# A graph and attention network on one core: the normalised features stay in SBUF, and the first loop turns them from there, one step ahead

## The reference

```python
xn = _layernorm(x, axis=-1)
x = x + _L0_gnn_ref(xn, src, dst, edge_weight, ...) + _L0_mix_ref(xn[None], ...)[0]

# _L0_gnn_ref: xn @ W_self + segment_sum((xn @ W_neighbor)[src] * weight, dst) + bias
# _L0_mix_ref:
qkv = x @ W_qkv + b_qkv
q, k, v = jnp.split(qkv, 3, axis=2)      # q and k less their means
k2 = _l2_normalize(k * k / (k2s + EPS_DIV), axis=-2)   # over the nodes
q2 = _l2_normalize(q * q / (q2s + EPS_DIV), axis=-1)
kv = jnp.einsum('bnc,bnd->bcd', k2, v)
attn = v + jnp.einsum('bnc,bcd->bnd', q2, kv) / math.sqrt(N)
return attn @ W_out + b_out
```

## Time and profile before

| what | before |
|---|---|
| median of 3 runs | 3417.4 us (3412.79 to 3418.47) |
| the profiled execution | 3412.11 us, of this a span of 3410.5 us |
| busy: PE / DVE / ACT / POOL | 2484.1 / 1166.1 / 1083.1 / 587.4 us |
| PE busy from 0 to 50, 50 to 100, 100 to 150, 150 to 200 us | 0.00, 3.04, 26.12, 14.71 us |
| PE busy from 500 to 550 us | 47.62 us |
| first instruction of the graph sums' stage on DVE | 454.33 us |
| mean granted TensorE clock | 0.838 of full speed (2.4 GHz; the lower level of 1.2 GHz stands as 0.50) |

### The profile page before, as it was taken

One profiled execution on the slowest core, in us unless ns is written; L12 is line 12 of the kernel. 1 busy time (PEld: TensorE's weight loads), 2 busy tenths in 40 slices (PEclk: granted clock), 3 DMA queues, 4 the chain that ended last, 5 costly groups with the idle time before them and its releaser, 6 DMA issues.

```text
span 3410.5 us, 39172 instructions
## 1 busy us (share of the span) xinstructions
PE 2484.1 (73%) x11905; PEld 1986.4 (58%) x11906; DVE 1166.1 (34%) x2489; ACT 1083.1 (32%) x1985; POOL 587.4 (17%) x482
## 2 busy tenths in 40 slices
PE   0455579987967869787489926588787877853887
PEld 0223368876756757666378814366565655642776
DVE  3233357765253544532100043202333233221111
ACT  2312157775544445542133321001111111111222
POOL 1222001010010010102112100131212121212544
PEclk9777669999879789897689968798788878776999
DMA  3222011111011010112322132321212112023443
GB/s 109 72 91 80 34 41 41 40 47 39 27 43 37 24 56 28 42 37 82 94 77 74 53 116 100 88 65 33 70 42 73 51 52 62 25 73 87 82 93 63
DMA packets 168994, 208.46 MB, mean 61 GB/s; under 512 B 59830, under 2 KB 137399, under 8 KB 168860
## 3 DMA queue, kind: packets, MB, share of 16 engines
q0 software_dynamic: 75168, 89.11, 11.3%
q1 hardware_dynamic: 80342, 88.80, 8.1%
q10 hardware_dynamic: 13350, 28.87, 2.4%
HBM read 114.91 MB, written 93.74 MB: 61 GB/s over the span
## 4 chain that ended last, share of the span: by engine, by line
PE 57%; DMA 15%; another core or an unknown queue 14%; DVE 4%; SPq 3%; ACT 3%; issue 3%; ACTq 0%; DVEq 0%; POOL 0%; POOLq 0%
PE bank L708 53%; DMA agg_rows<-agg_t 8%; PE bank L714 4%; DMA arena<-agg_rows 3%; DMA counts<-count_a 1%; SPq L478 1%; ACT t L1099 1%; SPq L395 1%; SPq L471 1%; DMA rows_b<-arena 0%; SPq L476 0%; DMA out_rows<-arena,ids_cur 0%; DVE arena L1824 0%; DMA w_qc<-counts 0%
## 5 line engine op out<-in xcount | busy, mean ns | idle before, releaser
L708 PE MATMUL bank<-xg,w_adj 125*125 125x256 f32 (+1 forms) x2500 | 664.6, 405 | 10.7 <-POOLq L71 10.7
L708 PE MATMUL bank<-arena,row_hot 128*125 128x100 f32 x3200 | 448.8, 289 | 115.3 <-remote 70.9
L708 PEld LDWEIGHTS bank<-arena,row_hot 128*125 128x125 f32 x3200 | 443.5, 206 | 152.0 <-issue 130.5
L708 PEld LDWEIGHTS bank<-xg,w_adj 125*125 125x125 f32 x2500 | 463.8, 198 | 77.0 <-issue 11.9
L714 PE MATMUL bank<-ident,arena 125*128 125x125 f32 x700 | 158.4, 351 | 409.2 <-remote 307.0
L714 PEld LDWEIGHTS bank<-ident,arena 125*128 125x128 f32 x700 | 95.8, 174 | 469.3 <-issue 464.6
L708 PE MATMUL bank<-t,w_h 128*128 128x250 f32 (+1 forms) x1184 | 329.6, 432 | 16.2 <-remote 10.6
L1137 ACT ACTIVATE w_adj<-bank 125x200 f32<-125x200 f32 x400 | 213.3, 533 | 334.7 <-PE bank L708 324.8
L1505 DVE TENSOR_TENSOR row_hot<-iota_all,arena 128x2000 f32<-128x2000 f32 x100 | 223.9, 2239 | 270.2 <-PE bank L708 263.9
L708 PEld LDWEIGHTS bank<-t,w_h 128*128 128x128 f32 x1184 | 232.4, 202 | 110.4 <-issue 58.7
L708 PE MATMUL bank<-w_adj,arena 128*125 128x256 f32 x1024 | 241.8, 394 | 0.0
(11 more groups left out here) (312 smaller groups left out, 2989.7 us busy)
## 6 DMA issues: line engine op xcount, KB each, us to landing
sorted_in<-pad_rows POOLq DMA_DIRECT2D x16, 878.4 KB, 16.8
arena<-sorted_in SPq DMA_DIRECT2D x49, 251.0 KB
counts<-count_a ACTq DMA_DIRECT2D x13, 781.2 KB
count_a<-counts POOLq DMA_DIRECT2D x13, 781.2 KB, 7.7
counts<-w_qc ACTq DMA_DIRECT2D x12, 781.2 KB
w_qc<-counts POOLq DMA_DIRECT2D x12, 781.2 KB, 6.1
arena<-rows_b SPq DMA_DIRECT2D x5, 1875.0 KB
w_adj<-in_L_ffn_Wd POOLq DMA_DIRECT2D x8, 1024.0 KB
```

The lines of the kernel that those rows point to most:

```text
L708: return pe.matmul(o, w, r, start=first, stop=last, skip_group_check=not check)
```

## The change

The normalisation writes into `xg` instead of in place; the scratch of the tables moves from `xg` to `w_adj`, and the ones in `xg`'s last column are written at POOL's start. `feat0` is still stored, from `xg`, but neither the steps' rows nor `xg` are loaded from it. `l_x` becomes five semaphores, one a slice. SP issues the tables' stores ahead of the weights. PE turns a step's rows out of `xg` during the step before it (`t4` has four planes, two for each of two steps) and works on the next step's first two blocks ahead of this step's sums. DVE takes the first guesses before the loop, finds the first edges in step 0, and makes one group of slots after each of steps 1 to 4 and one at the end. The copy of `tail_n` moves from the preparation to `dense_or_tails`. The loop of the normalisation is written out.

```diff
-CSR = {3: (0,), 4: (1, 2), 5: (3, 4)}
+CSR = {1: (0,), 2: (1,), 3: (2,), 4: (3,), 5: (4,)}
...
         def scratch(rows, at, n):
-            return xg[0:rows, at:at + n, :].rearrange("p a b -> p (a b)")
+            return w_adj[0:rows, 257 * at:257 * (at + n)]
...
+            take(sp, tables_made)
+            sp.dma_start(tile_min, st_min[:, :]).then_inc(tables_stored, 16)
+            sp.dma_start(tile_max, st_max[:, :]).then_inc(tables_stored, 16)
             sp.dma_start(wqkvs[:, :, 0:3 * D], wview(a["L0_mix_W_qkv"])).then_inc(l_w0, 16)
...
-            take(sp, tables_made)
-            sp.dma_start(tile_min, st_min[:, :]).then_inc(tables_stored, 16)
-            sp.dma_start(tile_max, st_max[:, :]).then_inc(tables_stored, 16)
             sp.wait_ge(tables_stored, 32)
...
-                sp.dma_start(fv[:, G * i:G * i + G, :], x_big[:, G * i:G * i + G, :]).then_inc(feat0_stored, 16)
+                sp.dma_start(fv[:, G * i:G * i + G, :], xg[:, G * i:G * i + G, 0:D]).then_inc(feat0_stored, 16)
...
-            sp.wait_ge(feat0_stored, 80)
 
             def x_rows(s):
                 take(sp, xa_used)
-                sp.dma_start(y, rows(feat0, s)).then_inc(xa_in, 16)
                 sp.dma_start(x1, rows(a["x"], s)).then_inc(xa_in, 16)
...
-            take(sp, xf_full)
-            sp.dma_start(xg[:, 0:NB, 0:D], by_part(feat0)).then_inc(xf_full, 16)
...
+            def heads(s, i):
+
+                if i < 2 or s == 0:
+                    pe.wait_ge(t_full, i + 1)
+                if i == (G - 1 if s == 0 else 2):
+                    pe.wait_ge(t_full, G)
+                    pe.sem_clear(t_full)
+                at = lambda c: t4[:, 2 * (s % 2) + c, B * i:B * i + B]
+                take(pe, h_free[i % 2])
+                for c in range(KC):
+                    last = mm(ps_h[i % 2][0:B, :], at(c), wqkvs[:, c, 0:512], c == 0, c == 1)
+                last.then_inc(h_dve[i % 2], 1)
+                take(pe, y_free[i % 2])
+                for c in range(KC):
+                    last = mm(ps_y[i % 2][0:B, :], at(c), wqkvs[:, c, 512:1024], c == 0, c == 1)
+                last.then_inc(y_dve[i % 2], 1)
+
+            turn_rows(xg[0:B, 0:G, :])
+            heads(0, 0)
+            heads(0, 1)
             for s in range(NS):
-                take(pe, v_full)
-                turn_rows(y)
-                for i in range(G):
-                    turned(i)
...
+                for i in range(2, G):
+                    heads(s, i)
+                    if s < NS - 1 and i == (G - 1 if s == 0 else 2):
+                        turn_rows(xg[0:B, G * s + G:G * s + 2 * G, :])
+                if s < NS - 1:
+                    heads(s + 1, 0)
+                    heads(s + 1, 1)
 
                 take(pe, k4_full)
...
+            copy_turned(2)
             for s in range(NS):
-                copy_turned(2)
+                if s < NS - 1:
+                    copy_turned(2, 2 * ((s + 1) % 2))
...
-            with dve.Fori(0, NS) as s:
-                for i in range(G):
-                    last = dve.bn_stats(bn6[:, i, :], flat(x_big[:, ds(s * G + i, 1), :]))
+            for s in range(NS):
+                dve.wait_ge(l_x[s], 16)
+                for i in range(G):
+                    last = dve.bn_stats(bn6[:, i, :], x_big[:, s * G + i, :])
...
-                    last = ts(rows_i, rows_i, mv[:, i, 0:1], rs[:, i:i + 1], ALU.subtract, ALU.mult)
+                    last = ts(xg[:, s * G + i, 0:D], x_big[:, s * G + i, :], mv[:, i, 0:1], rs[:, i:i + 1],
+                              ALU.subtract, ALU.mult)
...
-            dve.wait_ge(tables_loaded, 64)
-            chain(dve.tensor_copy(n_f[:, :], tail_n[:, :]))
...
-                take(dve, xa_in, 32)
-                dve.sem_inc(v_full, 1)
...
                 dve.sem_inc(act_in, 1)
+                take(dve, xa_in, 16)
                 chain(tt(row_a[:, :, 0:D], row_a[:, :, 0:D], x1, ALU.add))
...
-                if s == 0:
-                    first_tiles_of()
...
-                if s == 1:
+                if s == 0:
                     first_edges_of()
...
+            first_tiles_of()
             for s in range(NS):
                 attend0(s, s < NS - 1)
```

More of the change, by code:

```diff
@@ L268, in program @@
         t_min, t_max, t_msk, t_val, t_iot = (range_t[:, NT * i:NT * i + NT] for i in range(5))
-        l_x, l_edge, l_w0, l_wh, l_l1, l_c, l_bc, l_b1 = (
-            sem(n) for n in ("x_loaded", "edges_loaded", "w_mix0_loaded", "w_hid0_loaded", "w_layer1_loaded",
+        l_edge, l_w0, l_wh, l_l1, l_c, l_bc, l_b1 = (
+            sem(n) for n in ("edges_loaded", "w_mix0_loaded", "w_hid0_loaded", "w_layer1_loaded",
                              "w_c_loaded", "biases_c_loaded", "b1_loaded"))
+        l_x = [sem(f"x_loaded{s}") for s in range(NS)]
         const_full = sem("consts_made")
@@ L291, in program @@
         adj_in, adj_used = pair("adjacency_in"), pair("adjacency_used")
-        xf_full, graph_done, tables_free = sem("features0_loaded"), sem("graph_summed"), sem("projections_done")
+        graph_done, tables_free = sem("graph_summed"), sem("projections_done")
         l_w1 = sem("w_qkv1_loaded")
@@ L394, in _ @@
             for i in range(5):
-                sp.dma_start(x_big[:, 5 * i:5 * i + 5, :], xv[:, 5 * i:5 * i + 5, :]).then_inc(l_x, 16)
+                sp.dma_start(x_big[:, 5 * i:5 * i + 5, :], xv[:, 5 * i:5 * i + 5, :]).then_inc(l_x[i], 16)
+            take(sp, tables_made)
+            sp.dma_start(tile_min, st_min[:, :]).then_inc(tables_stored, 16)
+            sp.dma_start(tile_max, st_max[:, :]).then_inc(tables_stored, 16)
             sp.dma_start(wqkvs[:, :, 0:3 * D], wview(a["L0_mix_W_qkv"])).then_inc(l_w0, 16)
@@ L538, in _ @@
             chain(pool.tensor_copy(ident_b[:, :], ident[:, :]))
+            chain(pool.memset(xg[:, :, D:D + 1], 1.0))
             chain.restart()
@@ L552, in _ @@
             take(pool, first_tiles)
-            chain(pool.memset(xg[:, :, D:D + 1], 1.0))
-            chain.restart()
-            pool.sem_inc(xf_full, 1)
             tiles = a["dst"].rearrange("(t e) -> t e", e=B)
@@ L895, in _ @@
             zero(ps_kv, 512, True, False)
-            for s in range(NS):
-                take(pe, v_full)
-                turn_rows(y)
-                for i in range(G):
-                    turned(i)
-                    take(pe, h_free[i % 2])
-                    for c in range(KC):
-                        last = mm(ps_h[i % 2][0:B, :], at(c, i), wqkvs[:, c, 0:512], c == 0, c == 1)
-                    last.then_inc(h_dve[i % 2], 1)
-                    take(pe, y_free[i % 2])
-                    for c in range(KC):
-                        last = mm(ps_y[i % 2][0:B, :], at(c, i), wqkvs[:, c, 512:1024], c == 0, c == 1)
-                    last.then_inc(y_dve[i % 2], 1)
+            def heads(s, i):
[16 more added lines that the diff above has]
+            heads(0, 1)
+            for s in range(NS):
+                for i in range(2, G):
[5 more added lines that the diff above has]
+                    heads(s + 1, 1)
                 take(pe, k4_full)
@@ L945, in _ @@
             pe.wait_ge(tabs_ready, 2)
-            pe.wait_ge(xf_full, 16)
             first_adjacency()
@@ L1093, in _, with copy_turned @@
             chain = Chain(act, act_s)
-            def copy_turned(n):
+            def copy_turned(n, k=0):
                 for i in range(G):
                     take(act, t_act[i % 2])
-                    chain(act.activation(t4[:, 0:n, B * i:B * i + B],
+                    chain(act.activation(t4[:, k:k + n, B * i:B * i + B],
                                          ps_t[i % 2][:, 0:n * B].rearrange("p (k n) -> p k n", k=n), ACT.Copy))
@@ L1605, in dense_or_tails @@
             def dense_or_tails():
+                dve.wait_ge(tables_loaded, 64)
+                chain(dve.tensor_copy(n_f[:, :], tail_n[:, :]))
                 chain(dve.tensor_reduce(covered[:, NB:NB + 1], covered[:, 0:NB], AX.X, ALU.add))
```

2 lines of the change are left out of this document (removed).

## The result

The changed kernel takes 3335.2 us (median of 4 runs, 3330.04 to 3344.69) against 3415.1 us (4 runs, 3408.39 to 3418.47): a ratio of 0.977, 95% interval 0.974 to 0.980. The forecast was 3340 (3318 to 3366). The profiled execution took 3344.69 us, 3343.1 of it span. The graph sums' stage, which began at 454.33 us, now begins at 377.11, **77.2 us sooner**; the forecast's sum was 77.0, at 377.3.

A forecast was written before the change was run, and what follows sets the result against it. Up to 454 us a chain through all engines binds, TensorE mostly waiting. Start -29.5, copies +2.4, step 1 -30.7, steps 2 and 3 +8.0 each, step 4 -10.7, tail -24.5: 77.0 us saved, 3340 us forecast (3318 to 3366).

The forecast's parts named there:

- T(1): End of step 1's heads, forecast at 160.5 us; T(s) is the same for step s.
- Start: Up to the first heads: earlier tables' stores and no DRAM wait begin them at 93.3 us, 29.5 us earlier.
- The rival of stores that land no earlier: Tables' stores: loads ahead are as slow on all paths, the start loses 11.0 us, total 3351; chance 0.08.
- Copies ahead of the squares: Step 0: ScalarE copies step 1's turned rows before its squares, a loss of 2.4 us.
- Step 1's wait: Between step 0's sums and step 1's third block: TensorE waits for first edges until 145.0; by places -30.7 us.
- the rival of slower fetches: Edge lists: POOL's fetches take twice 37.5 us, first edges late by that, total 3377; chance 0.04.
- A step: Loop step with one slot group: 52.3 us, of which 15.5 is three blocks' heads, transposes and 2.4 slow start.
- The rival of 28 us: Heads ahead not hidden: banks freed late, sums pushed up to 7.0 us in four steps, total 3368; chance 0.07.
- The rival of a clock that holds: Sums: shorter pause keeps TensorE's clock high, up to -21 us over four steps, total 3319; chance 0.11.
- The transposes: Rival: transposes between heads lower the clock, slow start twice in four steps, +9.6 us, total 3350; chance 0.07.
- Tail: From T(4) to the graph sums' stage: fourth group at 345.5, a further group 12.1 us, stage at 377.3; -24.5 us.
- The stage behind: Everything after the graph sums' stage begins: unchanged at 2956 us.

The follow-up runs named there:

- e10: Changed kernel with the copy of the tail table back in the preparation, ahead of the weights' folding: stage start 381.2 us, median 3347.7 us, ratio 0.9809 to before.
- e1: Changed kernel with the stores of the two small tables back behind the seven weight loads: stage start 386.4 us, median 3346.8 us, ratio 0.9820 to before.
- e5: Kernel before with one edit, the two small tables' stores issued ahead of the seven weight loads: stage start 441.9 us, median 3405.1 us, ratio 0.9978.
- e3: Changed kernel with first edges found in step 1, slot groups behind steps 2, 3, 4 and two at the end: stage 367.0 us, median 3326.0 us.
- e8: Changed kernel with step 0's rows turned first, first guesses in step 0, first edges in step 1, all slots last: stage 357.6, median 3324.3 us.
- e2: Changed kernel with the next step's first two blocks issued behind this step's sums and slots: stage start 395.4 us, median 3359.6 us, ratio 0.9852 to before.
- e9: Changed kernel with 11 unread TensorE products filling each pause ahead of the sums, 27 in the last step: stage 384.0 us, median 3351.2 us.
- e12: e8 with 6 unread filling products in each pause ahead of the sums, 14 in the last: stage start 360.6 us, median 3321.3 us, ratio 0.9734 to before.
- e4: Changed kernel with one group of slots behind step 3, two behind step 4, two at the end: stage start 375.4 us, median 3329.5 us.
- e6: Changed kernel with the order of before, keeping only rows turned from SBUF, the late tail copy and the written-out loop: stage 398.8 us, median 3353.4 us.
- e11: e8 with the filling products of e9 (11 in each pause, 27 in the last): stage start 365.5 us, median 3322.5 us, ratio 0.9735 to before.

## Why the prediction was right

The mechanism was right, and the sum was right to 0.2 us at the stage's start, by steps that were right to some 2 us each. The 0.2 is luck, and so is a median within 5 us when executions scatter by 15: the steps' errors, up to 2.2 us late at T(1), cancelled. By its own steps:

- **Start: 93.3 forecast, 93.98 measured.** Two errors cancel. The stores landed 1.6 us later than I took (34.34 for 32.7): the last slice was issued by 21.2, but the first small store was then held at the queue for 5.24 us, and its landing came 7.7 us after the second's issue. Against it, the written-out loop of the normalisation takes 6.38 us a step (40.72 - 34.34), the loop before 6.8 (50.51 - 43.70); I had priced that part of the change at nothing, and by it ScalarE's count began 29.5 us behind the first normalisation instead of 31.1. The count ended at 90.98 (forecast 90.9), and the first copy began 0.6 us behind it, where I had taken nothing. ScalarE bound: VectorE waited 4.29 us for its count, and by e10 it had 3 us to spare (3.3 forecast). The rival of stores that land no earlier is out by e1 and e5.
- **The Trainium skill, "DMA: Bandwidth & Descriptors" (Why a DMA increments its semaphore by 16 and not by 1).** I had taken its rule on the engines, 5 of 16 for 125 rows, as speaking against a start before 32 us. The start at 34.3 agrees with that, and so does the mean busy share of the 16 transfer engines while only the slices moved, 0.34 from 6 to 26 us, which is 5.4 engines. No row shows whether it was the engines or the queue that held the stores.
- **Copies ahead of the squares, +2.4.** T(0) to the sums was 15.1 us (128.13 - 113.0), forecast 14.7.
- **Step 1's wait.** POOL's fetches ran from 92.89 to 130.70 (forecast 93.1 to 130.6), so the rival of slower fetches is out. The landing took 5.3 us after that, not 3.7, and the first heads behind it came at 147.25 instead of 145.0. The mis-sized term is the landing. e3 shows what this part of the change costs: 10 us.
- **A step: 52.3 forecast.** T(s) is here the start of the 32 rows and half of their 13.90 us, in step 4 the end of its 24 rows. T(1) to T(2) was 52.2, T(2) to T(3) 51.4. T(4) was 314.9, forecast 314.7: what step 1 came late was recovered by 0.9 us in step 3 and in step 4. The mis-sized term is the slow start: 2.4 us in step 1 as forecast, but 1.4, 1.2 and 1.2 in steps 2 to 4 (5.07, 4.91 and 11.73 us for rows that take 3.69 and 10.56 at full clock in e3 and e8).
- **Heads ahead are hidden.** The sums began 12.4 to 12.9 us after T in steps 1 to 4. e2 gives 6.7 us a step for the cover, forecast 7.0. The rival of 28 us is out.
- **The clock.** It had fallen to 0.50 at the sums in all five steps. The rival of a clock that holds was right in what it would do to the rows, and e9 makes it happen, but behind the pause of 5.4 us the clock was as low as behind the longer one. Its 21 us were too many: of its four steps, step 0 could give nothing, because TensorE stood behind its sums for the first edges anyway, and e9 gives some 15 us for the other sums, the last step's among them. No run shows how much would be left in this kernel with the filling at its right size; in e12, which has no slots in its loop, `row_a`'s store took the gain.
- **The transposes.** They ran at full clock (0.43 us a pair) and the 16 or 32 rows behind them at 1.00, in steps 0 to 3; step 4 turns nothing. So the rule of the Trainium skill, "TensorE: Matmul & The Clock Gate" (Part 4: PE-mode transpose), that transposes do not count for the clock as matmuls do, did nothing here in 2.6 us of transposes between heads; the slow start that I counted came once a step, ahead of the transposes: behind the wait for the first edges in step 1 (6.04 us for 8 rows that take 3.69), behind the slots' pauses from step 2 on (5.07 and 4.91).
- **Tail.** T(4) to the fourth group was 30.6 us (30.8), the next group 11.2 (12.1), from there to the stage 20.5 (19.7).
- **The stage behind.** I had said that I am wrong if it takes another time than 2956. It took 2966.0 in the profiled execution, and the other three executions had spans of 3328.5 to 3333.9, which with the same stage start leaves 2951 to 2957. Lined up instruction by instruction, TensorE is 77 to 78 us ahead of before up to 1095 us, 70 to 74 from 1300 to 2860 and 67 at the end. One of these steps can be read. From 1347.3 us TensorE runs 80 products with 8 columns (`wg`); they took 12.3 us before and 15.2 in the changed kernel, at a lower granted clock. They took 12.2 to 12.6 in e1, e4 and e10 too and 15.0 to 15.4 in the other nine, and the four executions with 12.2 to 12.6 are those with the shortest part behind (2955.8 to 2957.4; e3, with 15.4, follows at 2957.6). What decides which clock these rows get wasn't settled. The other steps go both ways from kernel to kernel, and I count them as scatter. Windows over the `wg` rows, before and in the changed kernel (the granted clock is the last number but two):

```profile
1347.30:1359.60 12.30, 12.30 (x82) 12.24 (x81) 5.01 (x4) 0.47 (x2) 1.82 (x2) 0.71 0.26 87
1273.00:1288.20 15.20, 15.20 (x82) 15.13 (x81) 4.94 (x4) 0.47 (x2) 1.82 (x2) 0.57 0.21 71
```

- **Sums and bounds.** The range of the forecast alone should read 3327 to 3359 by its own bounds, not 3325 to 3358, and a clock of 0.805 gives 3434, not 3430. Neither touches the forecast.

The parts nearly add up. From the kernel before it is 55.6 us to the resident rows (e6, with the moved tail copy and the written-out loop), from there 9.3 for the stores (e1) and 18.3 for the heads ahead (e2); the first edges in step 0 take 10.1 back (e3) and the groups of slots spread over the steps 2.7 (e4). That makes 70.4 of the 77.2. What is left lies in the first guesses and the turning done earlier, which no run separates, and in the place where the clock falls, by which e5 alone gained 3 us.

Of the versions tried, e8, e11 and e12 have the lowest ratios: the stage begins 11.6 to 19.5 us before the changed kernel's, and the medians are 11 to 14 us lower, but the intervals of the ratios overlap with the changed kernel's. That they are faster than it is shown for the stage's start and only likely for the total.

## What to carry to other kernels

Price a change along the one chain that ends last, and then look at what is next on it: filling the pause made the sums of e12 2 to 5 us shorter a step, and the store of a single-buffered tile took it back. A piece of work that is moved earlier must be checked against the transfer it waits for: the first edges, moved one step ahead, stood in front of their own data. And where executions scatter by more than the effect, compare the time of one marked instruction in the traces before comparing medians.

## What the runs showed of the hardware

- In the changed kernel the sums began at a granted clock of 0.50 behind a pause of 5.4 us, as before behind one of 12.3, although the heads ahead of both had run at 1.00 (step 2 of both kernels).
- In e9 and e11 nothing idled between the heads, the ones' rows and the wide rows. The ones' rows ran at 1.00 in every step, and the wide rows right behind them were granted 1.00 in some steps and 0.72 or 0.73 in others. What decides between the two wasn't settled. Pieces of pause of 0.3 to 0.8 us ahead of the ones' rows, in e12, left these at 1.00 as well. The windows of e11, the wide rows of steps 0 and 3:

```profile
128.70:133.30 4.60, 4.60 (x22) 3.73 (x21) 0.16 (x1) 0.00 (x0) 3.69 (x4) 1.00 0.46 143
...
245.50:251.80 6.30, 6.29 (x22) 4.91 (x21) 0.16 (x1) 0.00 (x0) 0.00 (x0) 0.73 0.28 108
```

- A step of the normalisation took 6.8 us in a hardware loop and 6.38 written out. The timeline of the kernel before has 0.67 us of idle time at a step's start where the changed one has 0.23:

```profile
50.51 1.73 DVE L1426 BATCH_NORM_STATS2 bn<-arena 125x6 f32 x5 [0.67 <-DVE arena L1436]
```
